# Second attention of a two-layer gated transformer block: eight score products in one run over four PSUM banks, queries and transposed rows through one bank, heads turned before the value products

## What is computed

```python
x = x + tanh(g_xattn[0]) * L0_xattn(layernorm(x), ctx, ctx)
x = x + tanh(g_ffn[0])   * L0_ffn(layernorm(x))
x = x + tanh(g_xattn[1]) * L1_xattn(layernorm(x), ctx, ctx)   # the stage of the change
x = x + tanh(g_ffn[1])   * L1_ffn(layernorm(x))
# L1_xattn, 16 heads of 16:
scores = einsum('bhqd,bhkd->bhqk', qh, kh) / 4
attn = softmax(scores, axis=-1)
return concat(einsum('bhqk,bhkd->bhqd', attn, vh)) @ Wo + bo
```

## Time and profile before

| | |
|---|---|
| median of 3 runs | 512.23 us (512.04 to 512.59) |
| span of the profiled execution, first to last instruction | 509.3 us |
| its own time beside the span | not recorded; the median is 2.9 us above the span |
| second attention, PE's first turn to last `heads_out` (163.56 to 290.73) | 127.2 us |
| busy in the whole span: PE, DVE, ACT, POOL | 94%, 75%, 51%, 29% |
| granted TensorE clock | 0.987 of full speed on average |

### The profile page before, as it was taken

How to read it: one execution, slowest core, us unless ns; L and a number is a source line. 1 busy time by engine, 2 the same in 40 slices (tenths; PEclk the granted TensorE clock), 3 DMA queues, 4 the chain that set the end, 5 groups by cost and what they waited for, 6 DMA issues and landing times.

```text
span 509.3 us, 8629 instructions
## 1 busy us (share of the span) xinstructions
PE 479.0 (94%) x3258; PEld 407.4 (80%) x3258; DVE 383.8 (75%) x771; ACT 258.0 (51%) x396; POOL 147.5 (29%) x123
## 2 busy tenths in 40 slices
PE   6999999999999999999999759999999999999991
PEld 4777789898887777777777528988999998999991
DVE  4799999899998867979778896557667575748441
ACT  2667788776865654555546314344434443444120
POOL 4364100010001202212013127115072827354253
PEclk9999999999999999999999979999999999999997
DMA  6523000000000001210311543035364737372041
GB/s 209 157 83 73 24 2 1 0 1 1 1 2 0 24 19 42 84 54 31 125 42 42 167 134 98 18 72 143 105 137 145 154 105 164 94 168 47 1 42 20
DMA packets 37166, 36.06 MB, mean 71 GB/s; under 512 B 6458, under 2 KB 35974, under 8 KB 36998
## 3 DMA queue, kind: packets, MB, share of 16 engines
q1 hardware_dynamic: 30665, 27.65, 17.6%
q0 software_dynamic: 6144, 7.66, 9.1%
q10 hardware_dynamic: 317, 0.21, 0.1%
HBM read 27.70 MB, written 8.39 MB: 71 GB/s over the span
## 4 chain that ended last, share of the span: by engine, by line
PE 65%; DVE 23%; issue 6%; ACT 3%; DMA 2%; POOL 1%; DVEq 0%; ACTq 0%; POOLq 0%
PE PS L1477 14%; PE PS L1478 14%; PE PS L1479 14%; PE PS L1893 5%; PE PS L1837 4%; PE PS L1750 3%; DVE tmp L1139 3%; DVE tmp L1128 3%; DVE hT_lo L1147 3%; PE PS L1497 3%; PE PS L1902 3%; DVE tmp L1116 1%; DVE xn L995 1%; DVE nmaxC L1170 1%; DVE tmp L1119 1%
## 5 line engine op out<-in xcount | busy, mean ns | idle before, releaser
L1477 PE MATMUL PS<-w_hi,hT_hi 128*128 128x256 f32 x384 | 110.3, 287 | 0.1
L1479 PE MATMUL PS<-w_hi,hT_lo 128*128 128x256 f32 x384 | 108.6, 283 | 0.0
L1478 PE MATMUL PS<-w_lo,hT_hi 128*128 128x256 f32 x384 | 108.6, 283 | 0.0
L939 ACT ACTIVATE tmp<-PS,biasT 128x512 f32<-128x512 f32 (+1 forms) x80 | 43.8, 600 | 111.0 <-PE PS L1479 111.0
L664 POOL DMA_INDIRECT out<-tmp,dst_idx x32 | 55.8, 1744 | 99.5 <-DVE tmp L1433 92.8
L1477 PE MATMUL PS<-xT_hi,w_hi 128*128 128x512 f32 (+1 forms) x224 | 81.1, 362 | 0.4 <-DVE xT_lo L1003 0.4
L1478 PE MATMUL PS<-xT_lo,w_hi 128*128 128x512 f32 (+1 forms) x224 | 80.7, 360 | 0.0
L1479 PE MATMUL PS<-xT_hi,w_lo 128*128 128x512 f32 (+1 forms) x224 | 80.5, 359 | 0.0
L1477 PEld LDWEIGHTS PS<-w_hi,hT_hi 128*128 128x128 f32 x384 | 73.4, 191 | 3.3 <-issue 2.3
L1478 PEld LDWEIGHTS PS<-w_lo,hT_hi 128*128 128x128 f32 x384 | 73.5, 191 | 0.8
L1479 PEld LDWEIGHTS PS<-w_hi,hT_lo 128*128 128x128 f32 x384 | 73.5, 191 | 0.0
(11 more groups left out here) (261 smaller groups left out, 865.8 us busy)
## 6 DMA issues: line engine op xcount, KB each, us to landing
w_raw<-in_L_ffn_w SPq DMA_DIRECT2D x72, 256.0 KB, 3.3
residual<-in_x SPq DMA_DIRECT2D x4, 512.0 KB, 5.5
out<-residual SPq DMA_DIRECT2D x3, 512.0 KB, 4.5
normed_rows<-xn SPq DMA_DIRECT2D x3, 512.0 KB, 2.9
kv<-in_L_ffn_b SPq DMA_DIRECT2D x1, 1024.0 KB, 6.6
tmp<-in_L_xattn_Wq SPq DMA_DIRECT2D x2, 256.0 KB, 5.6
out<-residual SPq DMA_DIRECT2D x2, 256.0 KB, 5.1
normed_rows<-xn SPq DMA_DIRECT2D x2, 256.0 KB, 4.0
```

The costliest lines, as they stand in the source:

```text
L939: act.activation(gD[:, G % 2, f, 0:P * n], H[:, G % 2, f, 0:P * n], ACT.Gelu, bias=biasT[:, col:col + 1]).then_inc(e_gelu, 1)
L1477: pe.matmul(o, lh, rh, start=start, stop=False, skip_group_check=skip)
L1478: pe.matmul(o, lh, rl, start=False, stop=False, skip_group_check=skip)
L1479: return pe.matmul(o, ll, rh, start=False, stop=stop, skip_group_check=skip)
```

## The change

The score pairs go to four banks, one for each 32-partition strip (`SC = PS[:, 1:5, :]`, the two halves m in the same bank behind each other), in one run of eight. The shift and the exponentials are then two equal parts, one for each half m: 8 heads each. The heads of tile t-2 are turned before the last two turns of weights, ahead of the values' products. The fourth score bank takes one of the two banks of `T`: for the second attention, chunks 1 to 3 put transposed rows and queries through bank 0 alone (`TQ`), in two halves each, one ahead of the values' products and one behind them, and ACT and DVE copy in halves.

```diff
-        SC = PS[:, 2:5, :]
+        TQ = PS[:, 0, :]
+        SC = PS[:, 1:5, :]
-        LG = PS[:, 1, 0:4 * NE].rearrange("p (t e) -> p t e", t=4)
+        LG = TQ[:, 0:4 * NE].rearrange("p (t e) -> p t e", t=4)
+        def scored(m):
+            return SC[:, :, 2 * KEYS * m:2 * KEYS * m + 2 * KEYS].rearrange("p b (h k) -> p b h k", h=2)
...
-            sp.wait_ge(c_scores, 3 * NT)
+            sp.wait_ge(c_scores, NT)
-                pool.wait_ge(c_max, t + 1)
+                pool.wait_ge(c_max, KD * t + 1)
...
 # ACT, iteration t
-                if t % 4 == 2 and c + 1 < NC:
-                    x_hi(round_of(2, c + 1))
-                if t % 4 == 3 and c + 1 < NC:
-                    copy_queries(c + 1)
-                if t in COLUMNS_AT:
-                    copy_logits(COLUMNS_AT[t])
...
-                    for i, heads in enumerate((slice(0, 12), slice(12, 16))):
-                        act.wait_ge(c_shift, 2 * t + 1 + i)
+                    for m in range(KD):
+                        heads = slice(HH * m, HH * m + HH)
+                        act.wait_ge(c_shift, KD * t + m + 1)
                         act.activation(eC[:, t % 2, heads, :], eC[:, t % 2, heads, :], ACT.Exp, scale=HD ** -0.5
                                        ).then_inc(c_exp, 1)
+                        if t % 4 == 2 and c + 1 < NC:
+                            x_hi_half(round_of(2, c + 1), m)
+                        if t % 4 == 3 and c + 1 < NC:
+                            copy_queries(c + 1, m)
+                        if m == 0 and t in COLUMNS_AT:
+                            copy_logits(COLUMNS_AT[t])
...
 # DVE, shift(t)
+                dve.wait_ge(c_scores, t + 1)
+                for m in range(KD):
+                    mx = nmaxC[:, t % 2, HH * m:HH * m + HH]
+                    dve.tensor_reduce(mx.rearrange("p (b h) -> p b h", h=2), scored(m), AX_X, ALU.max, negate=True
+                                      ).then_inc(c_max, 1)
+                    dve.wait_ge(c_max, KD * t + m + 1)
+                    dve.tensor_tensor(eC[:, t % 2, HH * m:HH * m + HH, :].rearrange("p (b h) k -> p b h k", h=2), scored(m),
+                                      bcast(mx.rearrange("p (b h) -> p b h", h=2).unsqueeze(3), [P, HH // 2, 2, KEYS]),
+                                      ALU.add).then_inc(c_shift, 1)
...
-                        x_lo(round_of(2, c + 1))
+                        x_lo_half(round_of(2, c + 1), 0)
...
+                if t % 4 == 2 and c + 1 < NC:
+                    x_lo_half(round_of(2, c + 1), 1)
...
 # PE
-            def scores(t, i):
+            def scores(t):
+                pe.wait_ge(q_copied, KD * (t // 4 + 1))
+                pe.wait_ge(c_shift, KD * t)
+                for m in range(KD):
+                    for strip in range(4):
+                        rows = slice(32 * strip, 32 * strip + 32)
+                        ins = pe.matmul(SC[:, strip, 2 * KEYS * m:2 * KEYS * m + 2 * KEYS].rearrange("p (h k) -> p h k", h=2),
+                                        qT[rows, m, here], Kpar[rows, m, b, :, :], start=True, stop=True)
...
             def turn_heads(s):
                 pe.wait_ge(c_conc, s + 1)
-                pe.wait_ge(c_copB, min(s + 2, NT))
-                if s >= 1:
-                    pe.wait_ge(c_wofree, s)
...
```

More of the change, by code:

```diff
@@ L428, in turns_to, with halves_of, half_turned @@
         def turns_to(r):
-            return sum(1 for q in range(r + 1) if q >= NR or ROUNDS[q][0] != 3)
+            return sum(halves_of(q) for q in range(r + 1))
+        def halves_of(r):
+            if r >= NR or ROUNDS[r][0] < 2 or ROUNDS[r] == (2, 0):
+                return 1
+            return 2 if ROUNDS[r][0] == 2 else 0
+        def half_turned(half):
+            return TQ.rearrange("p (k n) -> p k n", k=KD), slice(256 * half, 256 * half + 256)
         def step_of(G):
@@ L689, in x_hi, with x_hi_half @@
                 act.activation(xT_hi[:, r % 2, :, 0:n], T[:, :, 0:n], ACT.Copy).then_inc(xhi_ready, 1)
+            def x_hi_half(r, half):
+                act.wait_ge(tr_ready, turns_to(r) - 1 + half)
+                if half == 0:
+                    round_used(act, r - 2)
+                turned, columns = half_turned(half)
+                act.activation(xT_hi[:, r % 2, :, columns], turned, ACT.Copy).then_inc(xhi_ready, 1)
             def x_rest(r):
@@ L824, in ffn_output, with copy_queries @@
                 act.activation(xn[:, (c + 1) % 2, :, :].bitcast(I32), O, ACT.Copy, scale=256.0).then_inc(o_free, 1)
[L826 to L831, removed]
+            def copy_queries(c, m):
+                act.wait_ge(q_ready, KD * c + m + 1)
+                act.activation(qT[:, m, :], T[:, m, :] if c == 0 else TQ, ACT.Identity,
+                               bias=biasT[:, BQ1 + m:BQ1 + m + 1]).then_inc(q_copied, 1)
             act.activation(minus_ident, ident[:, :], ACT.Copy, scale=-1.0).then_inc(minus_ready, 1)
@@ L1003, in x_lo, with x_lo_half @@
                 dve.tensor_tensor(xT_lo[:, r % 2, :, 0:n], T[:, :, 0:n], xT_hi[:, r % 2, :, 0:n].bitcast(F32),
+                                  ALU.subtract).then_inc(xlo_ready, 1)
+            def x_lo_half(r, half):
+                dve.wait_ge(xhi_ready, turns_to(r) - NC - 1 + half)
+                turned, columns = half_turned(half)
+                dve.tensor_tensor(xT_lo[:, r % 2, :, columns], turned, xT_hi[:, r % 2, :, columns].bitcast(F32),
                                   ALU.subtract).then_inc(xlo_ready, 1)
@@ L1500, in transpose_x, with transpose_half @@
                 ins.then_inc(tr_ready, 1)
+            def transpose_half(r, half):
+                pe.wait_ge(xn_ready, r + 1)
+                T_free()
+                turned[0] += 1
+                o = half_turned(half)[0]
+                for i in range(2):
+                    for k in range(KD):
+                        ins = pe.transpose(o[:, k, P * i:P * i + P], xn[:, r % 2, 2 * half + i, P * k:P * k + P], ident[:, :])
+                ins.then_inc(tr_ready, 1)
             def xT(r, k, a=0, n=512):
@@ L1765, in _ @@
                     pe.wait_ge(late_split, 1)
-                    queries_of(0)
+                    for m in range(KD):
+                        queries_of(0, m)
                 if g == NB_PAIRS + 2:
                     pe.wait_ge(keys_placed, 4)
-                    pe.wait_ge(q_copied, KD)
                     pe.wait_ge(grid_ready, NB_PAIRS)
-                    for i in range(3):
-                        scores(0, i)
+                    scores(0)
                 if g < NB_PAIRS:
@@ L1849, in _ @@
                 if t < NT:
[L1850 to L1852 removed]
+                    scores(t)
                 if 1 <= t <= NT:
@@ L1868, in _ @@
                     ins.then_inc(c_trA, 1)
[L1869 to L1874 removed]
+                if t > NT:
+                    turn_heads(t - 2)
+                if t < NT and c + 1 < NC:
+                    if t % 4 == 2:
+                        transpose_half(round_of(2, c + 1), 0)
+                    if t % 4 == 3:
+                        queries_of(c + 1, 0)
                 if t in COLUMNS_AT:
@@ L1900, in _ @@
                     pe.wait_ge(c_ctcopied, s + 1)
+                    if t > NT:
+                        pe.wait_ge(c_wofree, s)
                     for k in range(KD):
@@ L1904, in _ @@
                     ins.then_inc(c_wo, 1)
+                if t % 4 == 2 and c + 1 < NC:
+                    transpose_half(round_of(2, c + 1), 1)
                 if t in COLUMNS_AT:
```

67 lines of the change are left out of this document (16 added, 51 removed).

## The result

| | before | after |
|---|---|---|
| median, measured side by side on one chip, 4 runs each | 512.41 us (512.04 to 512.93) | 499.86 us (499.09 to 500.75) |
| ratio | | 0.9755 [0.9741, 0.9768] |
| span of the profiled execution | 509.3 us | 497.7 us (its own time 499.68, 2.0 beside the span) |
| second attention, PE's first turn to last `heads_out` | 163.56 to 290.73: 127.17 us | 162.78 to 277.87: 115.09 us |
| iteration 1, then 2 to 5, 6 to 9, 10 to 13, 14 to the end | 7.26, 32.70, 32.46, 32.44, 22.31 | 6.69, 28.00, 29.66, 29.26, 21.48 |

The account below looks back on a forecast made before the run. PE was taken to bound the kernel before, and DVE iterations 6 to 13 after. Gains of 0.4, 1.0, 5.1, 2.5, 3.4 and 1.0 make 13.4 us: span 495.9, plus 2.9 gives 498.8 us, range 494.6 to 503.5.

Parts of the forecast that it names:

- Scores in one run: PE's scores, second attention: one run of eight products takes 0.72 us, saving 1.00 us in each of iterations 1 to 15.
- the nearer of its two bounds: Score run: four strips cost nothing more than three, 0.72 us; the other bound had every product standing alone.
- The rival with strips one by one: Score run: strips do not overlap, every product runs alone, run takes 2.30 us, kernel 516.4 us; chance 0.03.
- The prediction's estimate by the figure of the Trainium skill: Score run: passes take 0.68 us instead of 0.52, 0.16 more per run; kernel 499.8 us instead of 498.8.
- Heads earlier: PE's product with `wo` no longer waits for ACT's copy of the turned heads: 0.27 us saved in iterations 2 to 16.
- Shift in halves: DVE's shift: 0.80 us per 616-column part; first exponential starts after 1.6 us instead of 2.7; 0.4 gained in iteration 1.
- The rival in which DVE reads four banks slower: DVE's shift: four-bank access costs more, or the chain closes; at 0.5 us in 11 tiles, 504.3 us; chance 0.13.
- Extras through one bank: Transposed rows and queries in halves: waits for the second halves hidden, unless DVE is late, then up to 0.5 us.
- The sum: Whole kernel: gains by stretch of iterations together 13.4 us, span 509.3 to 495.9, median 512.2 to 498.8 us.
- Behind the stage: After the last `heads_out`: everything follows it on DVE and moves with it, so no further gain or loss.
- DVE bounds 6 to 13, PE 2 to 5: Four-iteration windows: PE sets 27.6 us in 2 to 5, DVE 30.0 in 6 to 9 and 29.0 in 10 to 13.
- The 1.4 us of idle time on DVE: Iterations 3, 7, 11: PE needs 7.0 us until `heads_out` can run, DVE 5.6, so DVE idles 1.4 us.

Follow-up runs that it names:

- E1: Changed kernel with the heads of tile t-2 turned late again, between the eighth and ninth value product; 507.50 us against 511.98 for the kernel before.
- E9: E1 with ACT copying the turned heads behind its first exponential and the first half of its extras; 502.87 us against 512.59 for the kernel before.
- E5: Changed kernel with one more unused DVE statistics instruction (0.33 us) in each of iterations 6 to 13; 501.78 us against 512.78 for the kernel before.
- E6: Changed kernel with two more unused DVE statistics instructions in each of iterations 2 to 5; 501.40 us, ratio 0.9766 to the kernel before.
- E11: Changed kernel with normalised rows of the second attention's chunks 1 to 3 written by ACT instead of DVE; 503.98 us against 512.59 before.
- E12: Changed kernel with the edits of E10 and E11 together; 504.02 us against 512.59 for the kernel before.
- E3: Changed kernel with PE turning the heads twice in iterations 6 to 13, 1.75 us more work; 500.72 us against 511.98 for the kernel before.
- E4: Changed kernel with PE turning the heads three times in iterations 2 to 5, 1.75 us more work; 501.19 us, ratio 0.9781 to the kernel before.
- E2: Kernel before with only the heads turned early, ahead of the last two turns of weights, scores still in three sets; 511.32 us against 511.98.
- E7: Changed kernel with the product with `wo` ahead of the second half of the queries in iterations 3, 7, 11; 501.95 us against 512.78 before.
- E10: Changed kernel with the queries' first half behind the values' products and second half behind `wo`; 501.42 us against 512.59 for the kernel before.

## Why the prediction came out right, step by step

- **Scores in one run.** Predicted 0.72 us, measured 0.73, with eight products on four strips. The sum had taken the nearer of its two bounds, that four strips cost no more than three, and that bound holds. The rival with strips one by one (2.30) is out. The prediction's estimate by the figure of the Trainium skill ("TensorE: Matmul & The Clock Gate", Part 3), 3.07 times for four row strips, put the figure on the passes alone and gave a run of 0.88; the trace does not agree with that estimate. It does not settle the figure itself: no run has the eight products one by one, and against the 2.30 that the prediction worked out for that case, entering and leaving included, 0.73 is 3.15 times.
- **Heads earlier.** What was predicted to happen is in the profile: `wo` in 0.90, and a single wait for the copy. The price of that part, 0.27 in each iteration, was wrong. It was costed as one wait of `wo`, and of ACT the prediction said only that its halved copies stand "at an engine that is half busy", priced at nothing; what waits in ACT's queue behind the copy of the heads was not asked. E1 shows that without it the change keeps only 4.5 us of its 12.5: ACT's queue is in order, and the copy of the heads held up the exponentials and the copies of the queries, on whose single bank PE had become dependent. By E9 the order of that queue is worth 5.6 us, and 3.0 remain. This is luck: the forecast was saved because the change moves both things at once.
- **Shift in halves.** Predicted 0.80 for each part, measured 0.79 and 0.80, from four banks. The rival in which DVE reads four banks slower is out. PSUM Bottleneck in the Trainium skill's "TensorEngine Tiling (Array Packing)" warns of another thing, that emptying PSUM may become the bottleneck once TensorE is faster. The trace agrees with that in part: DVE, which empties the score banks, rose to 91 and 92% busy in two windows and has the chain in iterations 5, 6, 8 and 9, by its own amount of work and not by slower reads.
- **Extras through one bank.** Said to be hidden unless DVE is late, then up to 0.5. DVE was late twice: PE waited 0.68 in iteration 7 for the low part of the rows, 1.0 with iteration 11; and 0.56 in iteration 2, where DVE's residual of 1.27 us stands ahead of the low part. The prediction had left that instruction out of its account of the wait, and this wait is about what the window 2 to 5 fell short by (4.7 for 5.1).
- **The sum.** Predicted gains by stretch against measured: start 0.4 and 0.8; iteration 1 1.0 and 0.6; 2 to 5 5.1 and 4.7; 6 to 9 2.5 and 2.8; 10 to 13 3.4 and 3.2; 14 to the end 1.0 and 0.8. Together 13.4 and 12.9. Every term lies within about 0.4 us.
- **Behind the stage** it was 0 predicted and -1.3 in the profiled spans (12.9 gained to the last `heads_out`, 11.6 in all). Most of that is the profiled run of the kernel before. Every run with its span on record took 1.7 to 2.2 us beside it, so the span of 509.3 belongs to a run of some 511.4, 1.0 below that kernel's median; by medians (12.55) only 0.3 us are lost behind the stage. For the same reason the 2.9 that the forecast added to the span is no property of the program: it was 2.0 in the profiled run after. The part from the first expert product to the end differs by 1.8 us between the profiles of the changed kernel and its variants (200.6 to 202.4 us; 200.5 in the kernel before), and the longer low stretch of the clock does not sort them: 10.2 us at the low level go with 201.3 in one profile of the changed kernel, 6.8 with 202.3 in the other. The first expert product came 18.1 us behind the last `heads_out` before and 18.5 in both profiles after, but 18.1 in E5, E6, E11 and E12 too; that is not explained.
- **What bounds.** "DVE bounds 6 to 13, PE 2 to 5" gave the right lengths from a picture that is too coarse. E3 agrees with it, E5 in its total but not in its place, E4 in half, E6 not. The chain runs on DVE in iterations 5, 6, 8, 9 and the start of 10, and on PE in 7, where the queries stand ahead of the values, and from the second turns of 10 to the `wo` of 13. The 1.4 us of idle time on DVE that the prediction put into 7 and 11 belongs to such crossings: DVE waits 4.9 us for `wo` and 2.5 for the values in the stage. DVE's backlog passes from one window into the next, which a budget by window cannot show.

## What to carry to other kernels

Ask of every wait that a change makes or removes what stands behind the waiting instruction in its engine's queue; here the place of one copy of 0.38 us on an engine busy for half its time was worth 5.6 us, and giving that engine 5 us more work cost 4, up to 1.5 of it by the clock. Where a change shares a buffer more tightly and reorders the work that empties it, test the parts apart before trusting a price for either: 4.5 and 0.7 us (2.5 at best) alone were 12.5 together. And where two engines are both above 90% in a loop whose iterations differ, follow the chain through all of them: the busy share did not tell which of the two set the time, and work added in one iteration came due in a later one.

## What the runs showed of the hardware

In five of fourteen profiled runs TensorE's clock fell inside the busy stage, each time near a single short wait of PE. In E2, E5, E6, E11 and E12 the granted clock went from 1.00 (2.4 GHz) to about 0.5 (1.2 GHz) for some 3.4 us, from 0.5 us before the end of the wait (E12, 2.35 us idle) to 2.2 us behind it (E2). In E2 the stretch was 1.00 us, in an iteration that otherwise kept PE busy. E2's timeline in iteration 3, from that stretch on (L1834 turns, L1477 to L1479 queries):

```profile
180.47 0.63 PE L1834 MATMUL PS<-ident,tmp 128*128 128x128 f32 x4 [1.00 <-DVE tmp L1221]
...
183.47 0.63 PE L1479 MATMUL PS<-xT_hi,wq_lo 128*128 128x512 f32 x1
183.89 0.63 PE L1477 MATMUL PS<-xT_hi,wq_hi 128*128 128x512 f32 x1
...
186.53 0.39 PE L1478 MATMUL PS<-xT_lo,wq_hi 128*128 128x512 f32 x1
186.76 0.40 PE L1479 MATMUL PS<-xT_hi,wq_lo 128*128 128x512 f32 x1
```

A 512-column product stands 0.42 from the next at the low level and 0.23 at the high one, so 3.4 us at the low level delay PE by some 1.5 us (an estimate from these rows), more than the wait itself. The changed kernel, E1, E3, E4, E7, E9 and E10 had single waits of 1.1 to 1.7 us in the stage and kept 1.00, and so did the second waits of 2.39 and 2.35 us in E11 and E12. So a wait's length alone does not decide it. That the wait is the cause is suggested by where the clock falls, not shown, and what decides is left open. For a kernel like this one it means that two kernels with as long a wait can differ by some 1.5 us, and that a single profiled run should be held against the times of the others.
